# The last layer's weight split: high parts on ScalarE, low parts on GpSimd

## The chip, the cores and the metric

One core of one Trainium2 chip runs the whole program as one launch. The metric is the device time of the kernel in microseconds (us); shorter is better. Engines are called as in the profile: PE is TensorE, ACT is ScalarE, DVE is VectorE, POOL is GpSimd, and SPq is the queue from which SyncE issues transfers.

## The reference

Four layers run one after the other on x of 2 x 256 tokens by 512 columns. Each adds a cross attention and then a feed-forward block. The change touches only the last block, a feed-forward with 8-bit arithmetic and outlier columns:

```python
def _linear8bit(x, W, b):
    col_max = jnp.max(jnp.abs(x), axis=tuple(range(x.ndim - 1)))
    outlier = col_max > THRESHOLD
    x_in = jnp.where(outlier, 0.0, x)
    x_out = jnp.where(outlier, x, 0.0)
    y = _ste_quant_rows(x_in) @ _ste_quant_rows(W).T
    y = y + x_out @ W.T + b
    return y
h = _linear8bit(x, W1, b1)
return _linear8bit(h, W2, b2)
...
x = x + _L3_ffn_ref(_layernorm(x, axis=-1), L3_ffn_W1, L3_ffn_b1, L3_ffn_W2, L3_ffn_b2)
```

W1 is 2048 x 512 and W2 is 512 x 2048. The quantised product uses bf16 integers that were prepared earlier in the program. The outlier product `x_out @ W.T` is made in full precision.

## The kernel before

There is no scheduler: each engine runs a list of instructions that is written out by hand, and semaphores order the engines against each other. The last block is called f3 in the code.

A full-precision product is made of three passes. Each 512-wide operand is split into a high part (the value rounded to the matmul's format) and a low part (the value less its high part), and `passes` issues high x high, high x low and low x high; they are lines L326, L327 and L328. The activations' high parts come from ACT and their low parts from DVE. The weights of f3 come in eight chunks (cc = 0 to 7; 0 to 3 are W1, 4 to 7 are W2), each of 4 pieces of 128x512. Even chunks go to the buffers `wq_hi`/`wq_lo`, odd ones to `wo_hi`/`wo_lo`. Chunk 0 is split ahead of f3. Chunks 1 to 7 are split by POOL in `f3_pool`: `f3_split` makes the high part of a piece with a multiplication by one (L2065) and then its low part (L2067). POOL starts a chunk when the buffer of two chunks earlier is read for the last time: `out_full` counts the finished tiles of the first product, `used` those of the second.

PE's list (`f3_pe`) has the 16 tiles of the first outlier product, `out_first(j)`, each 12 matmuls into the banks ps_t; among them six of the 16 tiles of the integer product, `int_first(j)`, each 4 bf16 matmuls (L2145). Then 16 rounds follow, of which the first ten hold `int_first(6 + j)` and `out_second(j)`, and the last six only `out_second(j)`, 12 matmuls into ps_s. `int_first(j)` waits until DVE has read the integer tile of two before (`int_out`). `out_second(j)` waits for DVE's low part of activation tile j. Last come the 64 matmuls of the second integer product (L2192).

DVE's work on a tile is `tile(j)`, in this order: read the integer tile (L2299), keep the running maximum of two tiles before (`scale_kept`, L2296), add the two products (L2305), make the low part of the tile before (`outlier_lo(j - 1)`, L2270), and then the column maximum (L2309) and two masks (L2312, L2313).

ACT's list (`f3_act`) has `keep(j)`, which copies an outlier tile out of its bank (L2207), and `parts_of(j)`, which makes the high part `ho_hi` (L2213) and the magnitude `q_c` (L2216) of tile j and waits for the masks of tile j and, from tile 4 on, for `used` >= j - 3. `f3_norm_act` stands ahead of it and copies the turned, normalised x to `xF` (L2093).

Of the kernel before, what the change touches and what calls it, by code (L numbers as in the profile page):

```python
# [20 lines left out]
ALU = mybir.AluOpType  # L21
ACT = mybir.ActivationFunctionType
AX = mybir.AxisListType
F32 = mybir.dt.float32
# [43 lines left out]
def program(nc, A, out):  # L68
    ctx = ExitStack()
    with ctx:  # L70
# [4 lines left out]
        def at(name, shape, dt, kb):  # L75
            return nc.alloc_sbuf_tensor_at(name, shape, dt, offset=base + int(kb * KB))

        def sem(name):
            return ctx.enter_context(nc.semaphore(name))
# [6 lines left out]
        W = {"q": [at("wq_hi", [P, 4, 512], F32R, 64), at("wq_lo", [P, 4, 512], F32R, 72)],  # L86
             "o": [at("wo_hi", [P, 4, 512], F32R, 80), at("wo_lo", [P, 4, 512], F32R, 88)],
             "kv": [at("wkv_hi", [P, 4, 256], F32R, 96), at("wkv_lo", [P, 4, 256], F32R, 100)]}
# [159 lines left out]
        w_in = {r: sem(f"w_{r}_in") for r in ("q", "kv", "o", "f")}  # L248
        w_rdy = {r: sem(f"w_{r}_split") for r in ("q", "kv", "o", "f")}
# [123 lines left out]
        class Norm:  # L373
# [86 lines left out]
            def act(self, e):  # L460
                if self.i == 0:
                    for d in range(DK):
                        e.wait_ge(s_xfull, d + 1)
                        e.activation(xT[0][:, d, :], turn_banks[d][:, :], ACT.Copy).then_inc(s_xhi, 1)
                elif self.i == 7:
                    f3_norm_act(e)
                else:
                    turn_act(e, self.c.g, self.c.hi, xT, self.banks)
# [1121 lines left out]
        def f2_dve(e, link):  # L1590
# [30 lines left out]
            for half in range(2):  # L1621
# [9 lines left out]
        s3 = {n: sem(f"l3_{n}") for n in ("S", "max", "exp", "rec", "T", "thi", "tlo", "pv", "spread", "scaled", "ohi", "olo", "zero", "sel",  # L1631
                                         "job_full", "job_hi", "job_out")}
# [46 lines left out]
        L3_JOBS = len(jobs3)  # L1679
# [259 lines left out]
        def l3_dve(e, link):  # L1939
# [37 lines left out]
            for k in slots3:  # L1977
# [29 lines left out]
                for j in ended3.get(k - 1, ()):  # L2007
# [4 lines left out]
        cf = START["f3"]  # L2012
        s4 = {n: sem(f"f3_{n}") for n in ("x_mask", "x_kept",
                                         "out_full", "out_kept", "int_full", "int_out", "row_full", "row_out", "largest", "diag",
                                         "x_int", "summed", "masks", "h_scaled", "h_int", "h_int_dve", "kept_max", "magnitude", "x_magnitude", "hi", "lo", "used", "acc", "finished", "added", "dequantised", "outliers_added",
                                         "x_staged")}
        INT_BEHIND = {7: 0, 9: 1, 11: 2, 12: 3, 13: 4, 14: 5}
        EARLY = len(INT_BEHIND)
# [3 lines left out]
        def raw_of(cc):  # L2022

            return RAW["f"] if cc >= 2 and cc % 2 == 0 else RAW["o"]
# [33 lines left out]
        def f3_split(e, cc, piece):  # L2058
            role = "qo"[cc % 2]
            n = (cf.q, cf.o)[cc % 2] + cc // 2  # L2060
            if piece == 0:
                e.wait_ge(w_in[role], 16 * n + 16)
            w = raw_of(cc)[:, piece, :]
            hi, lo = W[role][0][:, piece, :], W[role][1][:, piece, :]
            e.tensor_tensor(hi, w, one[:, 0:1].to_broadcast([P, 512]), ALU.mult).then_inc(w_rdy[role], 1)  # L2065
            e.wait_ge(w_rdy[role], 8 * n + 2 * piece + 1)
            e.tensor_tensor(lo, w, hi.bitcast(F32), ALU.subtract).then_inc(w_rdy[role], 1)  # L2067

        def f3_pool(e):
            for cc in range(1, 8):  # L2070
                if cc == 1:
                    e.wait_ge(s3["job_full"], L3_JOBS)
                elif cc < 6:
                    e.wait_ge(s4["out_full"], 4 * (cc - 1))
                else:
                    e.wait_ge(s4["used"], 4 * (cc - 5))
                for piece in range(4):
                    f3_split(e, cc, piece)
            for i, t in enumerate(POOL_OUT):
                e.wait_ge(s4["dequantised"], i + 1)  # L2080
                e.tensor_tensor(x[:, t, :], x[:, t, :], q_c[:, t, :], ALU.add).then_inc(s4["added"], 1)
# [3 lines left out]
        acc_i = [ps_t[0][:, :], ps_t[1][:, :], ps_t[2][:, :], ps_o[:, :]]  # L2085

        def f3_norm_act(e):
            def hi(d):
                e.wait_ge(s4["x_mask"], 2 * d + 2)
                e.activation(xT[0][:, d, :], xF[:, d, :], ACT.Copy, scale=q_mo[:, d:d + 1]).then_inc(g_hi, 1)  # L2090
            for d in range(DK):
                e.wait_ge(g_full, cf.g - 4 + d + 1)
                e.activation(xF[:, d, :], turn_banks[d][:, :], ACT.Copy).then_inc(s4["x_kept"], 1)  # L2093
                if d:
                    hi(d - 1)
            hi(DK - 1)
# [99 lines left out]
        def f3_act(e):  # L2196
            for d in range(DK):
                e.activation(q_xm[:, d, :], xF[:, d, :], ACT.Abs, scale=q_mi[:, d:d + 1]).then_inc(s4["x_magnitude"], 1)
            e.wait_ge(s_lay, LAY["f3"])

            def row_copy(full, dst, bank):
                e.wait_ge(s4["row_full"], full)
                e.activation(dst[:, :], bank, ACT.Copy).then_inc(s4["row_out"], 1)

            def keep(j):
                e.wait_ge(s4["out_full"], j + 1)
                e.activation(h[:, j, :], out_bank[j % 2], ACT.Identity, bias=q_b1[:, j:j + 1]).then_inc(s4["out_kept"], 1)  # L2207

            def parts_of(j):
                e.wait_ge(s4["masks"], 2 * j + 2)  # L2210
                if j >= 4:
                    e.wait_ge(s4["used"], j - 3)
                e.activation(ho[0][:, j % 4, :], h[:, j, :], ACT.Copy, scale=q_mo[:, j:j + 1]).then_inc(s4["hi"], 1)  # L2213
                if j >= 4:
                    e.wait_ge(s4["kept_max"], j - 2)
                e.activation(q_c[:, j % 4, :], h[:, j, :], ACT.Abs, scale=q_mi[:, j:j + 1]).then_inc(s4["magnitude"], 1)  # L2216
            for j in range(4):
                keep(j)
            row_copy(3, q_srow, ring[3])
            row_copy(3, q_rrow, int_bank[0])  # L2220
            for j in range(4, 11):
                keep(j)
            parts_of(0)
            keep(11)
            keep(12)
            parts_of(1)
            keep(13)
            row_copy(4, q_s2row, ring[3])
            keep(14)
            parts_of(2)  # L2230
            keep(15)
            for j in range(3, HT):
                parts_of(j)
            row_copy(6, q_rrow, out_bank[1])
            n = 0
            for hb in range(HT):
                if hb in DVE_TILES:
                    continue
                n += 1
                e.wait_ge(s4["h_scaled"], n)  # L2240
                t = q_c[:, (n - 1) % 4, :]
                e.activation(t, t, ACT.Copy, bias=MAGIC).then_inc(s4["x_staged"], 1)
                e.wait_ge(s4["x_staged"], n)
                e.activation(hq[:, hb, :], t, ACT.Copy, bias=-MAGIC).then_inc(s4["h_int"], 1)
# [137 lines left out]
        def _(e):  # L2382
# [30 lines left out]
            l3_pool(e)  # L2413
            norms[7].pool(e)
            f3_pool(e)

        @block.tensor
# [25 lines left out]
        @block.scalar  # L2443
        def _(e):
            for b in range(B):
                e.wait_ge(s_ctx[b], 16)
                for d in range(DK):
                    c = slice(b * SK, (b + 1) * SK)
                    e.activation(cT[0][:, d, c], craw[:, d, c], ACT.Copy).then_inc(s_chi, 1)
                if b == 0:  # L2450
                    norms[0].act(e)
            a0.act(e)
            norms[1].act(e)
            f0_act(e)
# [134 lines left out]
```

## Time and profile before

| | |
|---|---|
| median of 3 runs | 2056.43 us (2055.41 to 2062.31) |
| profiled execution: its time | 2061.42 us |
| its span in the trace | 2059.6 us |
| last block, from the first outlier matmul to the end | 1914 to 2059.6 us |
| share of the span that PE is busy | 95% |

The profiled execution is one run of its own, so its time isn't one of the three. Times of single instructions below come from it, in us from the start of the span.

### The profile page before, as it was taken

How to read it: one execution, taken by the hardware profiler on the slowest of the kernel's cores; microseconds unless marked ns; L12 is line 12 of the kernel's file. 1: busy time of each engine (PE TensorE's matmuls, PEld its weight loads, DVE VectorE, ACT ScalarE, POOL GpSimd, SP SyncE). 2: the span in 40 equal slices, each digit the busy share in tenths (PEclk: the TensorE clock that was granted, in tenths of full speed). 3: DMA queues.
4: the chain of work that ended last, by engine and by line, in shares of the span. 5: the costliest groups of instructions: out<-in, count | busy, mean ns of one | idle time of the engine just before them, and what ended most of it. 6: DMA issues, size and time to landing. Idle time of an engine off the chain costs nothing.

```text
span 2059.6 us, 32190 instructions
## 1 busy us (share of the span) xinstructions
PE 1959.6 (95%) x11708; PEld 1662.0 (81%) x11716; DVE 1480.3 (72%) x2999; ACT 1112.6 (54%) x2315; POOL 843.1 (41%) x822
## 2 busy tenths in 40 slices
PE   6999999999899999988999999999998999998887
PEld 4888888888778888877888889889887877876665
DVE  6777777777676777666667767667676477777798
ACT  4756666566325555641556556555554167776333
POOL 6554654542633122043443253343215733151762
PEclk9999999999999999999999999999999999999899
DMA  4101111010213232012111121111111200120210
GB/s 154 52 22 52 52 41 43 21 52 21 90 29 81 74 91 56 23 39 72 42 44 55 42 67 55 41 67 60 43 47 41 99 23 22 42 83 1 71 57 21
DMA packets 49053, 107.56 MB, mean 52 GB/s; under 512 B 18560, under 2 KB 28032, under 8 KB 41600
## 3 DMA queue, kind: packets, MB, share of 16 engines
q1 hardware_dynamic: 35072, 84.51, 12.1%
q10 hardware_dynamic: 13824, 20.98, 3.3%
q8 instruction: 96, 1.57, 0.3%
q14 instruction: 61, 0.50, 0.1%
HBM read 97.08 MB, written 5.24 MB: 50 GB/s over the span
## 4 chain that ended last, share of the span: by engine, by line
PE 85%; DVE 8%; issue 2%; ACT 2%; POOL 2%; DMA 1%; SPq 0%; ACTq 0%; DVEq 0%; POOLq 0%
PE ps_s L326 11%; PE ps_s L328 11%; PE ps_s L327 11%; PE ps_t L1112 8%; PE ps_t L326 7%; PE ps_t L328 6%; PE ps_t L327 6%; PE ps_o L326 5%; PE ps_o L328 4%; PE ps_o L327 4%; PE ps_o L1854 3%; PE ps_t L1885 2%; PE ps_s L1840 2%; PE ps_t L1119 1%; DVE l_pt_lo L1240 1%
## 5 line engine op out<-in xcount | busy, mean ns | idle before, releaser
L1167 ACT ACTIVATE l_pt_hi<-ps_t 128x512 fp32r<-128x512 f32 (+1 forms) x512 | 244.7, 515 | 319.3 <-PE ps_t L1112 294.5
L1232 DVE TENSOR_REDUCE nmax<-ps_s 128x1 f32<-128x768 f32 x192 | 183.7, 957 | 232.3 <-PE ps_s L328 230.4
L1240 DVE TENSOR_TENSOR l_pt_lo<-ps_t,l_pt_hi 128x512 fp32r<-128x512 f32 (+1 forms) x512 | 281.6, 581 | 5.3 <-ACT l_pt_hi L1167 5.3
L1198 ACT ACTIVATE l_p<-ps_s,nmax 128x768 f32<-128x768 f32 x192 | 173.6, 904 | 150.3 <-DVE nmax L1232 149.6
L1112 PE MATMUL ps_t<-ident,l_p 128*128 128x128 f32 x1664 | 237.9, 274 | 10.6 <-DVE l_pt_lo L1240 5.2
L326 PE MATMUL ps_o<-l_pt_hi,l_v_hi 128*128 128x256 f32 (+1 forms) x832 | 236.8, 285 | 5.8 <-DVE l_pt_lo L1240 5.8
L1112 PEld LDWEIGHTS ps_t<-ident,l_p 128*128 128x128 f32 x1664 | 197.9, 141 | 53.3 <-issue 11.5
L328 PE MATMUL ps_o<-l_pt_hi,l_v_lo 128*128 128x256 f32 (+1 forms) x832 | 235.0, 282 | 0.0
L327 PE MATMUL ps_o<-l_pt_lo,l_v_hi 128*128 128x256 f32 (+1 forms) x832 | 234.6, 282 | 0.0
L326 PE MATMUL ps_s<-l_k_hi,l_q_hi 128*128 128x512 f32 (+3 forms) x512 | 206.7, 404 | 1.3 <-ACT l_p L1198 1.2
L364 POOL TENSOR_TENSOR wo_hi<-raw_big,one 128x512 fp32r<-128x512 f32 (+2 forms) x100 | 103.5, 1035 | 193.5 <-PE ps_t L328 181.7
L328 PE MATMUL ps_s<-l_k_hi,l_q_lo 128*128 128x512 f32 (+3 forms) x512 | 180.7, 353 | 0.0
L327 PE MATMUL ps_s<-l_k_lo,l_q_hi 128*128 128x512 f32 (+3 forms) x512 | 180.2, 352 | 0.0
L326 PEld LDWEIGHTS ps_o<-l_pt_hi,l_v_hi 128*128 128x128 f32 (+1 forms) x832 | 152.7, 184 | 13.4 <-DVE l_pt_lo L1240 11.1
L327 PEld LDWEIGHTS ps_o<-l_pt_lo,l_v_hi 128*128 128x128 f32 (+1 forms) x832 | 152.7, 184 | 2.3
L328 PEld LDWEIGHTS ps_o<-l_pt_hi,l_v_lo 128*128 128x128 f32 (+1 forms) x832 | 152.8, 184 | 0.0
L364 POOL TENSOR_TENSOR wq_hi<-raw_big,one 128x512 fp32r<-128x512 f32 (+1 forms) x104 | 114.8, 1104 | 90.1 <-PE ps_t L328 55.2
L652 POOL TENSOR_TENSOR w_raw<-w_raw,w_row 128x512 f32<-128x512 f32 x32 | 41.5, 1296 | 259.9 <-DMA w_raw<-in_f_w 215.4
L1228 DVE CUSTOM_DVE_ANT_0 l_p<-ps_s,l_mask 128x512 f32<-128x512 f32 x128 | 87.8, 686 | 81.9 <-PE ps_s L328 81.2
L1189 ACT ACTIVATE l_p<-l_p,rinv 128x768 f32<-128x768 f32 (+1 forms) x160 | 136.2, 852 | 1.2 <-DVE rinv L1293 0.5
L366 POOL TENSOR_TENSOR wq_lo<-raw_big,wq_hi 128x512 fp32r<-128x512 f32 (+1 forms) x104 | 132.6, 1275 | 8.2
L1297 DVE TENSOR_SCALAR l_p<-l_p,rinv 128x768 f32<-128x768 f32 (+1 forms) x160 | 130.8, 818 | 5.7
(397 smaller groups left out, 5375.1 us busy)
## 6 DMA issues: line engine op xcount, KB each, us to landing
raw_big<-in_l_wq SPq DMA_DIRECT2D x18, 1024.0 KB, 4.8
raw_big<-in_l_wo SPq DMA_DIRECT2D x18, 1024.0 KB, 4.8
w_raw<-in_f_w ACTq DMA_DIRECT2D x32, 256.0 KB, 3.1
raw_big<-in_f_w SPq DMA_DIRECT2D x7, 1024.0 KB, 4.9
raw_kv<-in_l_wkv SPq DMA_DIRECT2D x12, 512.0 KB, 5.7
raw_f<-in_f_w SPq DMA_DIRECT2D x4, 1024.0 KB, 4.8
w_nat<-in_f_w1n ACTq DMA_DIRECT2D x16, 256.0 KB, 3.0
w_nat<-in_f_w2n ACTq DMA_DIRECT2D x16, 256.0 KB, 3.0
```

Source lines behind the costliest of these rows:

```text
L326: pe.matmul(o, a[0], b[0], start=start, stop=False)
L327: pe.matmul(o, a[0], b[1], start=False, stop=False)
L328: return pe.matmul(o, a[1], b[0], start=False, stop=stop)
L364: pool.tensor_tensor(hi, w, one[0:parts, 0:1].to_broadcast([parts, cols]), ALU.mult).then_inc(w_rdy[role], 1)
L366: pool.tensor_tensor(lo, w, hi.bitcast(F32), ALU.subtract).then_inc(w_rdy[role], 1)
L1112: mm = e.transpose(o[:, kk * P:(kk + 1) * P], sp.p[:, k % 3, at:at + P], ident[:, :])
L1167: e.activation(sp.pt[u % 2][0][:, k0:k0 + nk, qt * P:(qt + 1) * P], ps_t[p % 2][:, 0:nk * P].rearrange("p (k q) -> p k q", q=P), ACT.Copy) ...
L1189: e.activation(pr, pr, ACT.Copy, scale=rinv[:, (k - 1) % TILES:(k - 1) % TILES + 1]).then_inc(s_scl[0], 1)
L1198: e.activation(sp.p[:, k % 3, :], sp.p[:, k % 3, :] if l.rope else self.scores_out(k), ACT.Exp, bias=nmax[:, i:i + 1], scale=-1.0 if l.rop ...
L1232: e.tensor_reduce(nmax[:, i:i + 1], self.scores_out(k), AX.X, ALU.max, negate=True).then_inc(s_max, 1)
L1240: e.tensor_tensor(pt[1], ps_t[p % 2][:, 0:nk * P].rearrange("p (k q) -> p k q", q=P), pt[0].bitcast(F32), ALU.subtract).then_inc(s_tlo, 1)
L1297: e.tensor_scalar(pr, pr, rinv[:, i:i + 1], None, ALU.mult).then_inc(s_scl[1], 1)
```

## The change

ACT gets a new function, `f3_weight_hi(e, cc)`, which makes the four high parts of chunk cc as copies and waits for what POOL used to wait for. It is called at seven places in ACT's list. POOL keeps the low parts, waits for each high part (`weight_hi`), and signals twice as much, so that every reader's count stays the same.

```diff
--- before.py
+++ after.py
...
@@ -2066,16 +2066,25 @@
             e.wait_ge(w_rdy[role], 8 * n + 2 * piece + 1)
             e.tensor_tensor(lo, w, hi.bitcast(F32), ALU.subtract).then_inc(w_rdy[role], 1)
 
+        def f3_weight_hi(e, cc):
+            role = "qo"[cc % 2]
+            if cc == 1:
+                e.wait_ge(s3["job_full"], L3_JOBS)
+            elif cc < 6:
+                e.wait_ge(s4["out_full"], 4 * (cc - 1))
+            else:
+                e.wait_ge(s4["used"], 4 * (cc - 5))
+            e.wait_ge(w_in[role], 16 * ((cf.q, cf.o)[cc % 2] + cc // 2) + 16)
+            for piece in range(4):
+                e.activation(W[role][0][:, piece, :], raw_of(cc)[:, piece, :], ACT.Copy).then_inc(s4["weight_hi"], 1)
+
         def f3_pool(e):
             for cc in range(1, 8):
-                if cc == 1:
-                    e.wait_ge(s3["job_full"], L3_JOBS)
-                elif cc < 6:
-                    e.wait_ge(s4["out_full"], 4 * (cc - 1))
-                else:
-                    e.wait_ge(s4["used"], 4 * (cc - 5))
+                role = "qo"[cc % 2]
                 for piece in range(4):
-                    f3_split(e, cc, piece)
+                    e.wait_ge(s4["weight_hi"], 4 * (cc - 1) + piece + 1)
+                    e.tensor_tensor(W[role][1][:, piece, :], raw_of(cc)[:, piece, :],
+                                    W[role][0][:, piece, :].bitcast(F32), ALU.subtract).then_inc(w_rdy[role], 2)
             for i, t in enumerate(POOL_OUT):
                 e.wait_ge(s4["dequantised"], i + 1)
                 e.tensor_tensor(x[:, t, :], x[:, t, :], q_c[:, t, :], ALU.add).then_inc(s4["added"], 1)
@@ -2085,6 +2094,8 @@
         acc_i = [ps_t[0][:, :], ps_t[1][:, :], ps_t[2][:, :], ps_o[:, :]]
 
         def f3_norm_act(e):
+            f3_weight_hi(e, 1)
+
             def hi(d):
                 e.wait_ge(s4["x_mask"], 2 * d + 2)
                 e.activation(xT[0][:, d, :], xF[:, d, :], ACT.Copy, scale=q_mo[:, d:d + 1]).then_inc(g_hi, 1)
@@ -2218,10 +2229,15 @@
                 keep(j)
             row_copy(3, q_srow, ring[3])
             row_copy(3, q_rrow, int_bank[0])
-            for j in range(4, 11):
+            f3_weight_hi(e, 2)
+            for j in range(4, 8):
+                keep(j)
+            f3_weight_hi(e, 3)
+            for j in range(8, 11):
                 keep(j)
             parts_of(0)
             keep(11)
+            f3_weight_hi(e, 4)
             keep(12)
             parts_of(1)
             keep(13)
@@ -2229,8 +2245,11 @@
             keep(14)
             parts_of(2)
             keep(15)
+            f3_weight_hi(e, 5)
             for j in range(3, HT):
                 parts_of(j)
+                if j in (7, 11):
+                    f3_weight_hi(e, 6 + j // 8)
             row_copy(6, q_rrow, out_bank[1])
             n = 0
             for hb in range(HT):
```

ACT's list around tiles 14, 15 and 3 is one of the two places that matter below. `h` is what `keep` writes, `ho_hi` and `q_c` are what `parts_of` writes. Before:

```order
L2207 ACTIVATE h<-ps_t,q_b_183 128x512 [waits f3_out_full]
L2213 ACTIVATE ho_hi<-h,q_mo 128x512 [waits f3_masks]
L2216 ACTIVATE q_c<-h,q_mi 128x512
L2207 ACTIVATE h<-ps_t,q_b_183 128x512 [waits f3_out_full]
L2213 ACTIVATE ho_hi<-h,q_mo 128x512 [waits f3_masks]
L2216 ACTIVATE q_c<-h,q_mi 128x512
L2213 ACTIVATE ho_hi<-h,q_mo 128x512 [waits f3_used,f3_masks]
```

The same place in ACT's list of the changed kernel, where L2218 is `keep` and L2224 and L2227 are `parts_of`:

```order
L2218 ACTIVATE h<-ps_t,q_b_183 128x512 [waits f3_out_full]
L2224 ACTIVATE ho_hi<-h,q_mo 128x512 [waits f3_masks]
L2227 ACTIVATE q_c<-h,q_mi 128x512
L2218 ACTIVATE h<-ps_t,q_b_183 128x512 [waits f3_out_full]
L2079 ACTIVATE wo_hi<-raw_big 128x512 [waits w_o_in,f3_out_full]
L2079 ACTIVATE wo_hi<-raw_big 128x512 x3
L2224 ACTIVATE ho_hi<-h,q_mo 128x512 [waits f3_masks]
L2227 ACTIVATE q_c<-h,q_mi 128x512
L2224 ACTIVATE ho_hi<-h,q_mo 128x512 [waits f3_used,f3_masks]
```

The four copies of chunk 5 now stand between `keep(15)` and `parts_of(3)`.

POOL's list at chunk 5, before:

```order
L2065 TENSOR_TENSOR wo_hi<-raw_big,one 128x512 [waits w_o_in,f3_out_full]
L2067 TENSOR_TENSOR wo_lo<-raw_big,wo_hi 128x512 [waits w_o_split]
L2065 TENSOR_TENSOR wo_hi<-raw_big,one 128x512
L2067 TENSOR_TENSOR wo_lo<-raw_big,wo_hi 128x512 [waits w_o_split]
L2065 TENSOR_TENSOR wo_hi<-raw_big,one 128x512
L2067 TENSOR_TENSOR wo_lo<-raw_big,wo_hi 128x512 [waits w_o_split]
L2065 TENSOR_TENSOR wo_hi<-raw_big,one 128x512
L2067 TENSOR_TENSOR wo_lo<-raw_big,wo_hi 128x512 [waits w_o_split]
```

POOL's whole part of f3's weights in the changed kernel, chunks 1 to 7:

```order
L2086 TENSOR_TENSOR wo_lo<-raw_big,wo_hi 128x512 [waits f3_weight_hi,xn_ready]
L2086 TENSOR_TENSOR wo_lo<-raw_big,wo_hi 128x512 [waits f3_weight_hi] x3
L2086 TENSOR_TENSOR wq_lo<-raw_f,wq_hi 128x512 [waits f3_weight_hi] x4
L2086 TENSOR_TENSOR wo_lo<-raw_big,wo_hi 128x512 [waits f3_weight_hi] x4
L2086 TENSOR_TENSOR wq_lo<-raw_f,wq_hi 128x512 [waits f3_weight_hi] x4
L2086 TENSOR_TENSOR wo_lo<-raw_big,wo_hi 128x512 [waits f3_weight_hi] x4
L2086 TENSOR_TENSOR wq_lo<-raw_f,wq_hi 128x512 [waits f3_weight_hi] x4
L2086 TENSOR_TENSOR wo_lo<-raw_big,wo_hi 128x512 [waits f3_weight_hi] x4
```

Of POOL's 56 instructions on these weights 28 are left, one for each piece.

## Rows read from the trace of the kernel before

**Rows 1.** The page: engines' busy time, share of the span, instructions.
```profile
PE 1959.6 (95%) x11708; PEld 1662.0 (81%) x11716; DVE 1480.3 (72%) x2999; ACT 1112.6 (54%) x2315; POOL 843.1 (41%) x822
```

**Rows 2.** Busy time of each engine in three stretches of f3, granted clock.
```profile
core 0: us, PE busy (x) PEld busy (x) DVE busy (x) ACT busy (x) POOL busy (x), PEclk, DMA share, GB/s
1949.00:1967.00 18.00, 17.86 (x83) 13.23 (x84) 15.54 (x22) 6.31 (x11) 16.60 (x12) 1.00 0.18 59
1970.00:1982.20 12.20, 8.50 (x37) 5.62 (x37) 12.13 (x16) 4.58 (x7) 11.53 (x8) 1.00 0.04 18
1982.20:1989.20 7.00, 6.74 (x30) 4.76 (x30) 6.93 (x15) 1.34 (x2) 0.00 (x0) 1.00 0.47 153
```

**Rows 3.** Timeline of PE: start, duration; the integer tiles and the closing transposes.
```profile
1970.16 1.04 PE L2145 MATMUL ps_t<-xq,q_w 128*128 128x512 bf16 x4
...
1975.41 1.04 PE L2145 MATMUL ps_o<-xq,q_w 128*128 128x512 bf16 x4 [1.46 <-DVE q_t L2299]
...
1981.36 1.04 PE L2145 MATMUL ps_t<-xq,q_w 128*128 128x512 bf16 x3 [2.15 <-DVE q_t L2299]
...
1985.42 1.04 PE L2145 MATMUL ps_o<-xq,q_w 128*128 128x512 bf16 x4 [0.26 <-DVE q_t L2299]
...
1989.04 1.04 PE L2145 MATMUL ps_t<-xq,q_w 128*128 128x512 bf16 x4
...
1999.02 0.81 PE L2145 MATMUL ps_t<-xq,q_w 128*128 128x512 bf16 x3 [2.29 <-DVE q_t L2299]
...
2004.02 1.04 PE L2145 MATMUL ps_o<-xq,q_w 128*128 128x512 bf16 x4
...
2011.49 1.04 PE L2145 MATMUL ps_o<-xq,q_w 128*128 128x512 bf16 x3
...
2028.70 0.60 PE L2115 MATMUL ps_t<-ident,q_amx 128*128 128x128 f32 x4
```

**Rows 4.** Two DVE lines over f3: durations ns min/median/max.
```profile
L2296 DVE TENSOR_TENSOR q_amx<-q_c,q_amx x16: 679/968/1406, 1956.4 to 2026.5; 128x512 f32<-128x512 f32 x16
...
L2305 DVE TENSOR_TENSOR h<-q_t,h x16: 678/1280/1789, 1949.9 to 2022.9; 128x512 f32<-128x512 f32 x16
```

**Rows 5.** Timeline of DVE around tiles 5 to 8.
```profile
1974.62 0.74 DVE L2299 SCALAR_TENSOR_TENSOR q_t<-ps_o,q_sw,q_srow 128x512 f32<-128x512 f32 x1
...
1980.56 0.74 DVE L2299 SCALAR_TENSOR_TENSOR q_t<-ps_t,q_sw,q_srow 128x512 f32<-128x512 f32 x1
...
1984.63 0.74 DVE L2299 SCALAR_TENSOR_TENSOR q_t<-ps_o,q_sw,q_srow 128x512 f32<-128x512 f32 x1
...
1986.49 0.74 DVE L2270 SCALAR_TENSOR_TENSOR ho_lo<-h,q_mo,ho_hi 128x512 fp32r<-128x512 f32 x1
...
1987.99 0.74 DVE L2299 SCALAR_TENSOR_TENSOR q_t<-ps_t,q_sw,q_srow 128x512 f32<-128x512 f32 x1
```

**Rows 6.** Timeline of ACT and DVE at tile 3.
```profile
1970.75 0.71 ACT L2213 ACTIVATE ho_hi<-h,q_mo 128x512 fp32r<-128x512 f32 x1
...
1972.07 1.78 DVE L2270 SCALAR_TENSOR_TENSOR ho_lo<-h,q_mo,ho_hi 128x512 fp32r<-128x512 f32 x1
```

**Rows 7.** Timeline of ACT: four copies from SBUF; first instruction of f3.
```profile
9.66 2.19 ACT L2449 ACTIVATE cT_hi<-craw 128x512 fp32r<-128x512 f32 x4 [7.64 <-DMA craw<-in_ctxT]
...
1909.35 0.60 ACT L2093 ACTIVATE xF<-ps_t 128x512 f32<-128x512 f32 x1 [13.02 <-PE ps_t L487]
```

**Rows 8.** Timeline of POOL: one low part.
```profile
1930.46 1.28 POOL L2067 TENSOR_TENSOR wq_lo<-raw_f,wq_hi 128x512 fp32r<-128x512 f32 x1
```

**Rows 9.** ACT's waits in f3: total us, times, longest.
```profile
ACT h L2207 <- PE ps_t L328: 33.3, 16, 3.0
...
ACT ho_hi L2213 <- PE ps_s L328: 17.6, 6, 4.8
```

**Rows 10.** Timeline of DVE: first low part of x, at the start of f3.
```profile
1911.71 1.72 DVE L2101 SCALAR_TENSOR_TENSOR xT_lo<-xF,q_mo,xT_hi 128x512 fp32r<-128x512 f32 x1
```

**Rows 11.** Busy time and granted clock around integer tile 12.
```profile
2000.00:2003.40 3.40, 3.40 (x10) 2.68 (x9) 3.37 (x6) 0.00 (x0) 1.04 (x1) 0.52 0.00 0
```

More of the change, by code:

```diff
@@ L2014, in program @@
                                          "out_full", "out_kept", "int_full", "int_out", "row_full", "row_out", "largest", "diag",
-                                         "x_int", "summed", "masks", "h_scaled", "h_int", "h_int_dve", "kept_max", "magnitude", "x_magnitude", "hi", "lo", "used", "acc", "finished", "added", "dequantised", "outliers_added",
+                                         "x_int", "weight_hi", "summed", "masks", "h_scaled", "h_int", "h_int_dve", "kept_max", "magnitude", "x_magnitude", "hi", "lo", "used", "acc", "finished", "added", "dequantised", "outliers_added",
                                          "x_staged")}
```

## The prediction

> **What bounds the kernel now.** I read the page first: PE is busy for 95% of the span [rows 1], so only a place where PE waits can pay. Then the busy time by stretch, in f3 alone, since nothing else is touched. From 1949 to 1967 PE is busy 17.86 of 18 us, though POOL runs for 16.60 of them [rows 2]: there PE is the bound, and what POOL or DVE gain is worth nothing. From 1970.0 to 1982.2 PE is busy 8.50 of 12.2 us, and DVE 12.13, with POOL on for 11.53. From 1982.2 to 1989.2 POOL is silent, and PE is busy 6.74 of 7 us [rows 2]. So the rounds behind 1970 are bound by DVE while POOL works, and by PE while it rests.
>
> PE's timeline gives the size. A round with nothing to wait for takes 1989.04 - 1985.42 = 3.62 us [rows 3]. The ten integer tiles of the rounds start at 1970.16 to 2011.49, nine rounds apart, 41.33 us where 9 x 3.62 = 32.58 would do: PE loses 8.75 us. Three rows name DVE's read of an integer tile (L2299) as what ended the wait [rows 3]. The last six rounds have no integer tile and run on without a wait. 8.75 us is therefore the ceiling for this stage.
>
> Why DVE is slow there: its two adds take 0.68 us at best and 1.41 and 1.79 at worst [rows 4]. Tile 5 (1974.62 to 1980.56), with POOL on, takes 5.94 us; tile 7 (1984.63 to 1987.99), with POOL off, 3.36 [rows 5]. PE wants a tile every 3.62 us, so DVE is quick enough alone and too slow beside POOL. Under POOL it loses 2.58 of 5.94 us, 0.43 us for each us. The three chunks split in this stage (5, 6, 7) have POOL on for some 11.5 us each [rows 2], 34.5 us, so DVE loses about 15.
>
> **The change part by part.** Removed: 28 multiplications on POOL, 12 of them in the stage that counts. Left there are 12 lows, 1.28 us each undisturbed [rows 8]; beside a busy DVE I take 1.6, 6.4 us a chunk instead of 11.5. At the same 0.43 DVE loses 3 x 6.4 x 0.43 = 8.3 us instead of 15, so it gets about 6.7 back. PE gets only what of it lies where PE waits.
>
> That price is weighed against a rule. The Trainium skill (SBUF — State Buffer, "Who interferes with whom") says that a VectorE instruction with two SBUF inputs and a GpSimd instruction lock each other out for their whole length. By it a low can cost DVE its full duration; at 1.28 us that makes 12 x 1.28 = 15.4 us, and the relief would be nil. The rows lie between: of the 3.36 us of a tile some 1.9 (L2296, L2305 and L2270) go to instructions with two SBUF inputs, and lows that run beside the rest cost nothing.
>
> Added: 28 copies on ACT. Four copies of 128x512 out of SBUF took 2.19 us at the program's start [rows 7]; this price I use for each chunk. Six of the seven groups are covered. Chunk 1 stands where ACT sat idle for 13.02 us [rows 7]. Chunks 2, 3 and 4 stand in front of a `keep`, and ACT waited there for PE before all 16 of them, 33.3 us in total and up to 3.0 at once [rows 9]; an outlier tile is needed two tiles later, so even 1 us of delay would be hidden. Chunks 6 and 7 stand in front of a `parts_of` that waited for PE's `used`, 17.6 us in 6 waits [rows 9], 2.9 on average. Without that cover each would cost up to 2.2 us.
>
> Chunk 5 is not covered. It stands in front of `parts_of(3)`, which ran at 1970.75 without a wait, and DVE used its result at 1972.07 [rows 6]. Now `ho_hi` of tile 3 begins near 1970.75 + 2.19 = 1972.9 and ends 0.71 later, at 1973.65. DVE's low part of tile 3 moves from 1972.07 to 1973.65 or, if a POOL instruction is ahead of it, 1974.0. Queued behind it are the column maximum and masks of tile 4 and the read of integer tile 5: from the start of L2270 to the next L2299 it is 1987.99 - 1986.49 = 1.50 us undisturbed [rows 5], 1.9 with some of POOL. So that read starts at about 1975.9 instead of 1974.62, 1.3 us late, and PE's 1975.41 becomes 1976.7. Bounds: 0.4 (POOL out of the way at once) and 2.2 us (all four copies).
>
> Then the relief begins. POOL's four lows of chunk 5 end near 1977.4 instead of 1982.0. Tile 5 costs 3.36 + 1.5 x 0.43 = 4.0, so DVE reads tile 6 at 1979.9, and PE's round starts at 1980.7 instead of 1981.36: 0.6 ahead. The next is then bound by PE, 3.62 later at 1984.4 instead of 1985.42: 1.0 ahead. Rounds follow at 1988.0 and 1991.6. `used` for chunk 6 comes at 1988.0; `ho_hi` of tile 7 is done by 1989.0, and DVE reads tile 9 at 1989.0 + 1.50 = 1990.5. Chunk 6 lays 6.4 us of POOL on the next tile: 3.36 + 6.4 x 0.43 = 6.1, so tile 10 is read from 1996.6 and PE goes on at 1997.4 instead of 1999.02: 1.6 ahead.
>
> The next round cost 2004.02 - 1999.02 = 5.00 us [rows 3], 1.38 more than 3.62, because from 2000.0 to 2003.4 the granted clock was 0.52, TensorE's lower level of 1.2 GHz [rows 11]. PE had waited 2.29 us just before. Now it waits 1997.4 - (1991.6 + 3.62) = 2.2 us, against 1999.02 - 1992.66 - 3.62 = 2.7 worked out the same way before. Waits of 1.46 and 2.15 us [rows 3] had no such fall behind them. I take it that it doesn't come back, which adds 1.4: 3.0 ahead. Chunk 7 meets a DVE that is a tile ahead; 0.2 more. This stage gives 3.2 us.
>
> At the start of f3, x's first low part took 1.72 us beside POOL [rows 10], where the same kind of instruction takes 0.74 alone [rows 5]. POOL now has half the work there; of the 0.98 us I take 0.3, with 0 and 0.98 as bounds. Weight loads are issued earlier, since a chunk's split ends earlier; nothing waited for one.
>
> Sum: -3.2 - 0.3 = -3.5 us on a profiled execution of 2061.42 us, or 0.17%. That execution lies 5.0 above the median 2056.43, nearly all of it outside this question, so I apply the difference to the median: 2052.9 us. A measurement of this kernel can tell about 0.3%, 6.2 us, from no change.
>
> **The rivals.** (1) PE's waits all go: DVE gets more than 6.7 back, the delay at chunk 5 costs nothing, and the start gives all it can. -8.75 - 0.98 = -9.7, 2046.7 us. For it speaks that DVE alone needs 3.36 for PE's 3.62; against it that the lows still come in one burst a chunk. Half of this way (6.2 or more) would be measurable: 0.16.
>
> (2) The clock falls again behind the wait near 1996: 1.6 + 0.2 + 0.3 = 2.1 ahead, 2054.3 us; a chance of 0.3, beside 0.38 for the forecast itself. Both lie in the same class. The Trainium skill (TensorE: Matmul & The Clock Gate, "HAM oscillation — how this bites in real kernels") has waits of PE throw it back to the slow clock, which agrees with the trace as far as that fall after a wait goes.
>
> (3) Slower: ACT's queue. The copies of chunk 5 cost their full 2.2 us in front of tile 3, and the lows block DVE as much as highs and lows did, so that the relief of the rounds is nil. Then the end moves by +2.2 less 0.3, 2058.3 us. It decides where the relief up to the next PE-bound round is under the delay: I have 1.9 (from 1.3 behind to 0.6 ahead) against 1.3. Against it speaks that tile 7 was quick as soon as POOL stopped [rows 5], and POOL now stops earlier. The lock of the Trainium skill's SBUF — State Buffer page, above, would lead here. 0.12, and of this 0.05 beyond the measurable, if chunks 6 and 7 lose their cover too (up to 2.2 each, +6.3 in all).
>
> (4) The change does nothing, because the lows are as long as POOL's presence was: 2056.4, a chance of 0.04.
>
> **How the numbers follow.** The forecast, (2), (4) and the nearer part of (3) are within 0.3%: 0.38 + 0.3 + 0.04 + 0.07 = 0.79. Faster by over 0.3%: 0.16. Slower: 0.05. The range reaches from near rival (1) to near rival (3): 2047.5 to 2058.5.
>
> **What would show it.** Right: lows of 1.28 to 1.6 us on POOL, four a chunk, no highs; ACT's four copies in about 2.2 us; `ho_hi` of tile 3 some 2 us after `keep(15)`, with DVE idle for 1 to 2 us in front of its low part; DVE's adds at 0.68 us in more of the tiles; PE's waits in the rounds 5 to 6 us in total instead of 8.75. Wrong: DVE's tile beside lows still near 5.9 us, ACT waiting for a weight load, copies over 0.65 us apart, or a stretch at 0.5 of the clock in another place of f3, which costs or gives back 1.4 to 3 us.

## The result and the profile after

The changed kernel takes 2053.28 us (median of 20 runs, 2048.43 to 2057.46), the kernel before 2058.43 us in the runs beside it (20 runs, 2053.48 to 2062.31). The ratio is 0.9977 with a 95% interval of 0.9969 to 0.9984: 4.7 us or 0.23% faster (3.3 to 6.4 us). The forecast was 3.5 us, 0.17%. That the time itself was forecast at 2052.9 us, 0.4 from the measured one, is luck: it was worked out from 2056.43 us for the kernel before, which the 20 runs put at 2058.43. A second series of 10 runs gave 0.9982 (0.9973 to 0.9991).

The profiled execution after has a span of 2055.2 us and a time of 2057.14 us. Its page shows POOL's busy time down from 843.1 us [rows 1] to 805.5, and DVE's from 1480.3 to 1465.1, though DVE has the same instructions. This is the page's part 1, busy time, share of the span and instructions:

```profile
PE 1960.3 (95%) x11708; PEld 1662.8 (81%) x11716; DVE 1465.1 (71%) x2999; ACT 1126.2 (55%) x2343; POOL 805.5 (39%) x794
```

PE's timeline answers to [rows 3]; L487 is the first transpose of x, L326 the first outlier matmul, L2156 an integer tile, L2126 the closing transposes. Start, duration, and in brackets the idle time ahead with what ended it:

```profile
1909.24 2.82 PE L487 MATMUL ps_t<-ident,xn 128*128 128x128 f32 x12 [5.92 <-DVE xn L416]
...
1913.74 0.76 PE L326 MATMUL ps_t<-xT_hi,wq_hi 128*128 128x512 f32 x1 [0.82 <-DVE xT_lo L2112]
...
1940.21 0.81 PE L2156 MATMUL ps_t<-xq,q_w 128*128 128x512 bf16 x3
...
1968.37 1.04 PE L2156 MATMUL ps_t<-xq,q_w 128*128 128x512 bf16 x4
...
1974.38 1.11 PE L2156 MATMUL ps_o<-xq,q_w 128*128 128x512 bf16 x4 [2.22 <-DVE q_t L2318]
...
1979.60 1.04 PE L2156 MATMUL ps_t<-xq,q_w 128*128 128x512 bf16 x3
1983.21 1.04 PE L2156 MATMUL ps_o<-xq,q_w 128*128 128x512 bf16 x4
...
1996.14 0.81 PE L2156 MATMUL ps_t<-xq,q_w 128*128 128x512 bf16 x3 [1.84 <-DVE q_t L2318]
1999.56 1.04 PE L2156 MATMUL ps_o<-xq,q_w 128*128 128x512 bf16 x4
...
2006.85 1.04 PE L2156 MATMUL ps_o<-xq,q_w 128*128 128x512 bf16 x3
...
2024.10 0.60 PE L2126 MATMUL ps_t<-ident,q_amx 128*128 128x128 f32 x4
```

From integer tile 6 to the closing transposes it is 2024.10 - 1968.37 = 55.73 us, against 2028.70 - 1970.16 = 58.54 before [rows 3]: 2.8 us less. The nine rounds take 38.48 us, so the loss against 9 x 3.62 us is down from 8.75 to 5.9. The first two rounds are the odd ones: the first takes 6.01 us (5.25 before), the second 5.22 (5.95 before).

The timelines of ACT, POOL and DVE show why; L2079 is a group of ACT's copies of a chunk, L2224 `ho_hi`, L2086 POOL's lows, L2289 DVE's low part of a tile, L2318 its read of an integer tile, L2324 the add. They answer to [rows 5, 6]. ACT first:

```profile
1968.96 2.18 ACT L2079 ACTIVATE wo_hi<-raw_big 128x512 fp32r<-128x512 f32 x4
...
1971.04 0.71 ACT L2224 ACTIVATE ho_hi<-h,q_mo 128x512 fp32r<-128x512 f32 x1
```

POOL's lows in the same view:

```profile
1969.72 5.45 POOL L2086 TENSOR_TENSOR wo_lo<-raw_big,wo_hi 128x512 fp32r<-128x512 f32 x4 [9.07 <-ACT wo_hi L2079]
1989.11 6.36 POOL L2086 TENSOR_TENSOR wq_lo<-raw_f,wq_hi 128x512 fp32r<-128x512 f32 x4 [13.95 <-ACT wq_hi L2079]
```

And DVE's timeline at tile 3 and at the tile beside chunk 6:

```profile
1971.79 1.03 DVE L2289 SCALAR_TENSOR_TENSOR ho_lo<-h,q_mo,ho_hi 128x512 fp32r<-128x512 f32 x1 [2.27 <-ACT ho_hi L2224]
...
1989.38 0.74 DVE L2318 SCALAR_TENSOR_TENSOR q_t<-ps_o,q_sw,q_srow 128x512 f32<-128x512 f32 x1
...
1990.88 1.77 DVE L2324 TENSOR_TENSOR h<-q_t,h 128x512 f32<-128x512 f32 x1
...
1995.12 0.74 DVE L2318 SCALAR_TENSOR_TENSOR q_t<-ps_t,q_sw,q_srow 128x512 f32<-128x512 f32 x1
```

The four copies take 2.18 us and `ho_hi` of tile 3 stands right behind them; DVE idles 2.27 us for it. POOL is on for 5.45 and 6.36 us a chunk instead of 11.5 [rows 2]. Beside the lows of chunk 6 DVE's tile still takes 1995.12 - 1989.38 = 5.74 us: a tile full of lows is as slow as one beside highs and lows (5.94, [rows 5]), but it is one tile and not two.

The stage that surprised is the start of f3. From the first transpose to integer tile 0 it is 1940.21 - 1909.24 = 30.97 us, against 33.88 in the profile before; I had forecast a gain of 0.3.

**Two profiles of one kernel differ.** In every one of the 14 profiles the clock of PE falls to half (1.2 GHz) for stretches of a few us, and not at the same place. In this profile one stretch lies over the second round (the view of stretches: busy us of PE, PEld, DVE, ACT and POOL, the count of instructions behind each, then the granted clock, the DMA share and GB/s):

```profile
1976.00:1977.00 1.00, 1.00 (x4) 0.71 (x4) 1.00 (x3) 0.00 (x0) 0.00 (x0) 0.50 0.79 131
```

So I read every experiment by its stages, and by the clock in them.

| profile | A: transposes to integer tile 0 | B: rounds | C: from B's end to the end |
|---|---|---|---|
| before | 33.88 | 58.54 | 30.9 |
| before_again | 32.90 | 59.55 | 30.0 |
| after | 30.97 | 55.73 | 31.1 |
| after_again | 30.73 | 55.79 | 31.0 |
| chunk1_only | 30.95 | 58.43 | 29.9 |
| chunks567_only | 32.76 | 54.69 | 32.4 |
| parts3_first | 30.98 | 55.46 | 31.5 |
| lows_8_columns | 30.96 | 53.72 | 30.4 |
| pool_keeps_highs_too | 30.74 | 58.52 | 31.1 |
| pool_after_x_lows | 33.60 | 58.55 | 31.0 |
| piecewise | 30.75 | 53.75 | 30.4 |
| piecewise_again | 31.08 | 53.73 | 30.8 |
| piecewise_late_chunk1 | 35.40 | 53.72 | 29.9 |
| chunk5_in_halves | 30.73 | 53.72 | 32.3 |

Each is the difference of two starts in PE's timeline, as worked out above, in us; C is the span less the start of the closing transposes. The first transpose of x starts anywhere from 1901.0 to 1911.0 us in these profiles, after code that is the same in all of them. That spread, and the 2.5 us in C, are in every time; A and B are not touched by it. Where the row of a tile's integer matmuls reads x3 and 0.81 us instead of x4 and 1.04, the trace lacks its first matmul and the start reads 0.23 us late. This makes A 0.23 us too long in before, after, chunk1_only, chunks567_only, parts3_first and lows_8_columns: for the changed kernel 30.74 and 30.73 us are left in its two profiles.

### The profile page after: what moved, and what is told of

The parts are those of the page before. It is cut to its first block and busy times, and to the rows that moved or that the text cites. A ratio compares the mean times of both kernels' runs of the same rounds, so it can differ in the third digit from the quotient of the medians.

```text
span 2055.2 us, 32218 instructions
## 1 busy us (share of the span) xinstructions
PE 1960.3 (95%) x11708; PEld 1662.8 (81%) x11716; DVE 1465.1 (71%) x2999; ACT 1126.2 (55%) x2343; POOL 805.5 (39%) x794
## 5 line engine op out<-in xcount | busy, mean ns | idle before, releaser
L326 PE MATMUL ps_o<-l_pt_hi,l_v_hi 128*128 128x256 f32 (+1 forms) x832 | 236.3, 284 | 6.0 <-DVE l_pt_lo L1240 6.0
L326 PE MATMUL ps_s<-l_k_hi,l_q_hi 128*128 128x512 f32 (+3 forms) x512 | 206.5, 403 | 1.3 <-ACT l_p L1198 1.2
L326 PEld LDWEIGHTS ps_o<-l_pt_hi,l_v_hi 128*128 128x128 f32 (+1 forms) x832 | 152.3, 183 | 13.6 <-DVE l_pt_lo L1240 11.3
```

Of the source, the lines that this page charges most:

```text
L326: pe.matmul(o, a[0], b[0], start=start, stop=False)
```

## The experiments

**chunk1_only** and **chunks567_only** each keep part of the change. The edit (the second has `(5, 6, 7)`); other chunks are split by POOL as before:

```diff
+        ON_ACT = (1,)
+
         def f3_weight_hi(e, cc):
+            if cc not in ON_ACT:
+                return
...
+                if cc not in ON_ACT:
...
+                    for piece in range(4):
+                        f3_split(e, cc, piece)
+                    continue
```

> Only chunk 1's four highs are on ACT; chunks 2 to 7 are split by POOL as before. The profiled pair shows the first outlier stage (from the transposes of x to integer tile 0) 2.9 us shorter after the change. Theory A (POOL's highs at the start delayed x's low parts on DVE, worth about 0.3 us, and the rest of the 2.9 is where TensorE's slow stretch happened to lie): from the first transpose of x to integer tile 0 this kernel takes 0.3 to 1 us less than before at the same clock, and the time is 0 to 1.5 us under before. Theory B (chunk 1 alone brings the whole 2.9 us, by the clock or by DVE): the time is about 3 us under before, ratio 0.9985. The rounds keep all of their 8.75 us of waits in both.

> Only the highs of chunks 5, 6 and 7 are on ACT; chunks 1 to 4 are split by POOL as before. Theory A (the gain of the rounds comes from less POOL beside DVE): from integer tile 6 to the closing transposes 55.7 us as in the changed kernel, against 58.5 before, so 2.8 us less, ratio about 0.9986. Rival (the earlier chunks matter for the rounds too, since they let DVE run ahead): more than 57 us in the rounds.

Measured: 2056.89 us, ratio 0.9992 (0.9983 to 1.0001), and 2055.85 us, ratio 0.9991 (0.9982 to 1.0). By the clocks both are near the edge of what can be told; the stages are clear. Chunk 1 alone gives A = 30.95, the whole gain of the start, and leaves B at 58.43. Chunks 5 to 7 alone give B = 54.69, and leave A at 32.76. So the change has two parts that add up, and chunks 2 to 4 give nothing to B. For chunk 1 the truth lies between the theories: 1.8 us of A (32.76 - 30.95) are POOL's doing, more than the 0.3 to 1 of theory A and less than the whole 2.9 of theory B.

The gain of A can be followed step by step. In chunks567_only PE waits for each of x's low parts, with a full clock from the first outlier matmul on. PE's timeline at the start of f3:

```profile
1909.44 0.47 PE L326 MATMUL ps_t<-xT_hi,wq_hi 128*128 128x512 f32 x1 [1.77 <-DVE xT_lo L2126]
...
1910.85 0.50 PE L326 MATMUL ps_t<-xT_hi,wq_hi 128*128 128x512 f32 x1 [0.48 <-DVE xT_lo L2126]
...
1912.54 0.50 PE L326 MATMUL ps_t<-xT_hi,wq_hi 128*128 128x512 f32 x1 [0.72 <-DVE xT_lo L2126]
...
1913.99 0.50 PE L326 MATMUL ps_t<-xT_hi,wq_hi 128*128 128x512 f32 x1 [0.49 <-DVE xT_lo L2126]
```

The first matmul comes 1909.44 - 1904.00 = 5.44 us behind the first transpose; in the changed kernel it is 1913.74 - 1909.24 = 4.50. That is 0.94 us, nearly the whole of the upper bound of 0.98 that I had. The rest comes behind it. DVE's timeline of chunks567_only has x's four low parts, the last two in one row:

```profile
1907.59 1.71 DVE L2126 SCALAR_TENSOR_TENSOR xT_lo<-xF,q_mo,xT_hi 128x512 fp32r<-128x512 f32 x1
...
1910.06 0.74 DVE L2126 SCALAR_TENSOR_TENSOR xT_lo<-xF,q_mo,xT_hi 128x512 fp32r<-128x512 f32 x1
...
1911.56 2.38 DVE L2126 SCALAR_TENSOR_TENSOR xT_lo<-xF,q_mo,xT_hi 128x512 fp32r<-128x512 f32 x2
```

In the changed kernel they take 0.84, 0.93 and 1.62 us. So the second low part was not slow with all of POOL's work there, but the first, the third and the fourth were. The four maxima of x, which DVE makes next, take 3.17 us against 2.87. When PE transposes the maxima, the whole difference is there. The rows are from PE's timelines of chunks567_only and of chunk1_only:

```profile
1917.87 0.66 PE L2140 MATMUL ps_s<-ident,q_amx 128*128 128x128 f32 x4 [0.18 <-DVE q_amx L2311]
```

```profile
1923.02 0.66 PE L2140 MATMUL ps_s<-ident,q_amx 128*128 128x128 f32 x4
```

They stand 1917.87 - 1904.00 = 13.87 and 1923.02 - 1910.95 = 12.07 us behind the first transpose, 1.80 apart. In both profiles of the changed kernel it is 12.07 us too, wherever the slow stretch lies. And 1.1 us more of the first pair's 2.9 (33.88 - 32.76) is only where the slow stretch lay: the kernel before has been profiled twice, with 33.88 and 32.90.

This pair also mends a reading of mine. I had put the long round at integer tile 12 (5.00 us, [rows 3]) down to the slow clock there [rows 11]. In chunk1_only the same round has a full clock and takes 2003.73 - 1998.91 = 4.82 us, with a wait for DVE. This is the stretch of that round in chunk1_only, with the columns as above:

```profile
1998.90:2003.70 4.80, 3.57 (x15) 2.45 (x14) 4.77 (x8) 1.10 (x3) 1.98 (x2) 1.00 0.00 0
```

PE's timeline of the same profile, at the end of the round:

```profile
2003.73 1.04 PE L2170 MATMUL ps_o<-xq,q_w 128*128 128x512 bf16 x4 [1.24 <-DVE q_t L2332]
```

DVE bound that round too. The tiles' rows at 1999.02 [rows 3] and 1998.91 both lack their first matmul, so that the rounds are really 5.23 and 5.05 us: a slow stretch that fell where PE would wait anyway cost 0.2 us.

**lows_8_columns** takes the lows away as well, all but 8 columns of each in chunks 5 to 7:

```diff
-                    e.tensor_tensor(W[role][1][:, piece, :], raw_of(cc)[:, piece, :],
-                                    W[role][0][:, piece, :].bitcast(F32), ALU.subtract).then_inc(w_rdy[role], 2)
+                    n = 512 if cc < 5 else 8
+                    e.tensor_tensor(W[role][1][:, piece, 0:n], raw_of(cc)[:, piece, 0:n],
+                                    W[role][0][:, piece, 0:n].bitcast(F32), ALU.subtract).then_inc(w_rdy[role], 2)
```

> The changed kernel, but POOL makes only 8 of the 512 columns of each low part of chunks 5, 6 and 7, so that part of the low products is left out and POOL is all but gone from the rounds; ACT's copies stay. Theory A (POOL's presence is what slows DVE's tile): DVE's adds take 0.68 us in every tile, a tile 3.36 us, and of PE's waits only the one behind chunk 5's copies is left, about 1.5 us: 51.5 to 52.5 us from integer tile 6 to the closing transposes, against 55.7. Rival (ACT's copies hold up the tiles too, at chunks 6 and 7): over 53 us, with PE waits near integer tiles 11 to 13.

Measured: 2049.87 us, ratio 0.9959 (0.9946 to 0.9971), B = 53.72. One slow stretch lies in the second round, which takes 5.22 us for 3.62; without it B would be 52.1 by estimate, in the expected range. The view of the add's line (durations in ns, min/median/max):

```profile
L2325 DVE TENSOR_TENSOR h<-q_t,h x16: 682/684/1762, 1940.6 to 2008.3; 128x512 f32<-128x512 f32 x16
```

And the one wait of PE over 1 us in the rounds, in PE's timeline:

```profile
1970.10 1.04 PE L2157 MATMUL ps_o<-xq,q_w 128*128 128x512 bf16 x4 [1.94 <-DVE q_t L2319]
```

The median add is 684 ns, against 1280 before [rows 4]. What is left is the wait behind chunk 5's copies. ACT's copies of chunks 6 and 7 cost nothing, as forecast.

**pool_keeps_highs_too** gives POOL the highs back as doubles, with ACT's copies in place:

```diff
+                    if cc >= 5:
+                        e.tensor_tensor(W[role][1][:, piece, :], raw_of(cc)[:, piece, :],
+                                        one[:, 0:1].to_broadcast([P, 512]), ALU.mult).then_inc(s4["again"], 1)
+                        e.wait_ge(s4["again"], 4 * (cc - 5) + piece + 1)
```

> The changed kernel, in which POOL also repeats the high part of each piece of chunks 5, 6 and 7 (a multiplication by one of the same size, written where the low part goes a moment later). ACT's copies stay where they are. Theory A (what the rounds gain is POOL's missing half beside DVE): the relief goes, PE waits in rounds 2 and 3 and near integer tiles 12 and 13 as before, and with the delay of tile 3 by ACT's copies the rounds take 59 to 60.5 us at full clock, more than the 58.5 of before. Rival (the gain came from ACT making the highs sooner, not from POOL's absence): 54.7 to 56 us. The start keeps its gain in both.

Measured: 2058.1 us, ratio 0.9996 (0.9985 to 1.0008). B is 58.52, the value of before: with the highs on POOL again the whole gain of the rounds is gone, though ACT makes them as early as in the changed kernel. The rival falls. I had expected 59 to 60.5, the delay at tile 3 on top; it wasn't there in the sum: the second integer tile comes 5.87 us behind the first (5.25 in the kernel before), and the later rounds make up for it.

**parts3_first** asks for the price of the copies' place:

```diff
-            f3_weight_hi(e, 5)
-            for j in range(3, HT):
+            parts_of(3)
+            f3_weight_hi(e, 5)
+            for j in range(4, HT):
```

> The changed kernel with parts_of(3) ahead of chunk 5's copies. Theory A (the copies delayed DVE's low part of tile 3 and with it integer tile 7): DVE no longer idles 2.3 us there, the second round starts 1.5 to 2.2 us earlier relative to the first than 6.0 us, and the stage to the closing transposes is 1 to 2 us shorter than 55.7 us. Rival (POOL's lows would then stand beside DVE's low part and take it back): the stage stays within 0.4 us of 55.7.

Measured: 2053.11 us, ratio 0.9971 (0.9957 to 0.9984), B = 55.46. Theory A was half right. The second round now starts 3.65 us behind the first instead of 6.01, 2.4 earlier, but the wait stands one round later:

```profile
1973.87 1.04 PE L2156 MATMUL ps_t<-xq,q_w 128*128 128x512 bf16 x3 [1.96 <-DVE q_t L2319]
```

That is the burst of four lows, which now all stand beside DVE's tile. The stage gains 0.27 us, inside the rival's 0.4; a slow stretch lies in the third round here and in the second round of the changed kernel, so this is not a clean comparison. Without the stretches B would be some 53.9 us here (a round of 3.62 for 5.21) against the 54.69 of chunks567_only. By this estimate the order of `parts_of(3)` and the copies is worth 0.8 us: less than theory A, but more than the rival's 0.4.

**piecewise** (and **piecewise_again**, the same kernel) also spreads chunks 6 and 7:

```diff
+        def weight_hi_piece(e, cc, piece):
+            role = "qo"[cc % 2]
+            e.wait_ge(s4["used"], 4 * (cc - 6) + piece + 1)
...
-                if j in (7, 11):
-                    f3_weight_hi(e, 6 + j // 8)
+                if 4 <= j < 12:
+                    weight_hi_piece(e, 6 + (j - 4) // 4, j % 4)
```

> The changed kernel with parts_of(3) ahead of chunk 5's copies, and the copies of chunks 6 and 7 spread: one piece behind each of parts_of(4) to parts_of(11), as soon as its buffer is read out, so that POOL's lows come one per round. Theory A (a burst of four lows makes one DVE tile take 5.7 us, which PE must wait for; one low a tile costs DVE 0.4 to 1.1 us of the 3.64 that a round has, 3.36 are needed): the wait of 1.84 us at integer tile 12 goes, no round over 4.1 us but the third, 52 to 53.5 us for the rounds at full clock. Rival (one low a tile blocks DVE by up to a whole low, 1.28 us, so that every round is DVE-bound): 8 rounds of 4.2 to 4.6 us, 56 us or more.

> The kernel that spreads the copies, once more, beside the changed kernel in the same call. By the profiles its rounds are 2 to 2.6 us shorter than those of the changed kernel at equal clock, so its ratio should be some 0.001 under that one's: about 0.9965, and its first time of 0.9958 partly luck.

Measured: 2049.93 us, ratio 0.9958 (0.9943 to 0.9974), and 2053.47 us, ratio 0.9973 (0.9962 to 0.9983), beside after_again at 0.9982 in the runs next to it. B is 53.75 and 53.73: the wait at integer tile 12 is gone, the last six rounds take 3.64 or 3.65 us each, 2 us less than the changed kernel in both profiles. By the times alone the two kernels' intervals overlap, so that it beats the changed kernel is shown by the stage and only likely by the clock. I had expected 52 to 53.5 at full clock. What I missed stands in the second profile, where no slow stretch lies in the rounds:

```profile
1974.02 1.04 PE L2162 MATMUL ps_t<-xq,q_w 128*128 128x512 bf16 x4 [1.93 <-DVE q_t L2325]
...
1979.23 1.04 PE L2162 MATMUL ps_o<-xq,q_w 128*128 128x512 bf16 x4 [1.41 <-DVE q_t L2325]
```

The first pieces of chunk 6 follow right on chunk 5's burst, and DVE is bound for a second round.

**chunk5_in_halves** moves the pieces of chunks 6 and 7 one tile later and cuts that burst in two:

```diff
-            f3_weight_hi(e, 5)
+            weight_hi_piece(e, 5, 0)
+            weight_hi_piece(e, 5, 1)
...
+                if j == 4:
+                    weight_hi_piece(e, 5, 2)
+                    weight_hi_piece(e, 5, 3)
```

> As the kernel that spreads the copies of chunks 6 and 7, which come one tile later, and chunk 5's copies in two pairs, behind parts_of(3) and parts_of(4). Theory A (the wait of 2 us at integer tile 8 comes from four lows of chunk 5 in one burst): it falls to under 1 us, and the rounds take 51.5 to 52.5 us at full clock, up to 1.6 more where a slow stretch of the clock falls in them. Rival (the lows only move, and DVE has no slack left in rounds 2 to 6): the same loss appears as small waits over several rounds, and the stage is not shorter than 53.7 us less the slow stretch, 52.1.

Measured: 2053.62 us, ratio 0.9972 (0.9962 to 0.9982), B = 53.72. The wait did not shrink: POOL's two pairs of lows came 0.32 us apart and filled the same tile.

```profile
1968.01 3.00 POOL L2092 TENSOR_TENSOR wo_lo<-raw_big,wo_hi 128x512 fp32r<-128x512 f32 x2 [10.30 <-ACT wo_hi L2085]
1971.33 3.05 POOL L2092 TENSOR_TENSOR wo_lo<-raw_big,wo_hi 128x512 fp32r<-128x512 f32 x2 [0.32 <-ACT wo_hi L2085]
```

The next round, 5.21 us, has a slow stretch in this profile. DVE is busy for 4.48 us of it, against 5.17 of 5.21 in piecewise_again, so by estimate it would be 0.7 us shorter or more at full clock; no profile shows it, and it stays open.

**pool_after_x_lows** tries the start without ACT, from the kernel before:

```diff
                     e.wait_ge(s3["job_full"], L3_JOBS)
+                    e.wait_ge(g_free, cf.g)
```

> The kernel before, with one wait more: POOL begins chunk 1 only when DVE has made the four low parts of x. All highs stay on POOL, nothing is added to ACT. Theory A (the start was slow because POOL's instructions stood beside x's low parts): from the first transpose to the first outlier matmul 4.4 to 4.5 us instead of 5.45, and 30.9 us to integer tile 0 at full clock against 32.8, as with the highs on ACT; chunk 1 is still done in time. Rival (POOL now collides with the later maxima and DVE's rounding of x): less than 1 us of it remains. The rounds stay at 58.4 to 58.5 us.

Measured: 2062.64 us, ratio 1.0017 (1.0008 to 1.0026), which is 3.5 us slower. The first outlier matmul does come 4.49 us behind the first transpose, as theory A had it, but A is 33.60: the rival was right. POOL's chunk 1 now stands beside the four running maxima of x, which DVE makes next, and PE waits for them. DVE's timeline of pool_after_x_lows, and then PE's:

```profile
1913.38 5.92 DVE L2279 TENSOR_TENSOR q_amx<-q_xm,q_amx 128x512 f32<-128x512 f32 x4
```

```profile
1919.35 0.66 PE L2116 MATMUL ps_s<-ident,q_amx 128*128 128x128 f32 x4 [2.94 <-DVE q_amx L2279]
```

In the changed kernel the same four take 2.87 us, in DVE's timeline:

```profile
1918.38 2.87 DVE L2297 TENSOR_TENSOR q_amx<-q_xm,q_amx 128x512 f32<-128x512 f32 x4
```

The stages don't account for the 3.5 us: A is only 0.7 us longer than the 32.90 of before_again, and B is the same. The profiled execution is the fastest of the 11 of this kernel (2057.89 us); what the others lost besides is not shown.

**piecewise_late_chunk1** has the same wait on top of piecewise.

> As the kernel that spreads the copies, and POOL also waits for the four low parts of x before it begins chunk 1. Expected beside it: the first transpose to the first outlier matmul 0.1 us less (DVE's low part 0.74 instead of 0.84 us), to integer tile 0 0.1 to 0.3 us less, the rounds the same. By the rival (a later start of POOL pushes chunk 1's lows into other DVE work that counts) the stage to integer tile 0 is longer than 30.97.

Measured: 2054.1 us, ratio 0.998 (0.9969 to 0.9991), with A = 35.40 and B = 53.72: the rival again, PE waits 3.24 us for the maxima. Here a slow stretch lies right behind that wait (granted clock 0.50 from 1922 to 1924 us), which makes A longer than in pool_after_x_lows, where the clock was full. Where the lows stand matters as much as how many they are.

**before_again** and **after_again** are the two kernels unchanged.

> The kernel before, unchanged, for a second profile. Theory A (where TensorE's slow stretches lie differs from one execution to the next; the rest doesn't): 58.4 to 58.6 us for the rounds without a slow stretch, up to 1.6 more with one; 32.7 to 34 us from the first transpose to integer tile 0, by where the slow stretch lies.

> The changed kernel, unchanged, for a second profile and more times. Theory A: 54.7 us for the rounds without a slow stretch, 55.7 with one as in the first profile; 30.7 to 31 us from the first transpose to integer tile 0 wherever the slow stretch lies; ratio 0.9970 to 0.9985.

Measured: 2061.72 us in one run, and 2056.92 us, ratio 0.9982 (0.9973 to 0.9991). In before_again a slow stretch lies in the third round, so B is 59.55 and not 58.5, while the round at integer tile 12 takes 2005.16 - 2000.12 = 5.04 us at full clock. In after_again B is 55.79, with a slow stretch in the second round as in the first profile, and A is 30.73, as expected. The two stretches, with the columns as above:

```profile
1981.50:1986.80 5.30, 5.24 (x16) 3.70 (x16) 5.23 (x10) 0.72 (x2) 0.75 (x1) 0.68 0.56 202
2000.10:2005.20 5.10, 3.82 (x17) 2.61 (x18) 5.07 (x8) 1.40 (x4) 2.21 (x2) 1.00 0.00 0
```

## Why the prediction was right, point by point

**What bounds the stage** held. B's gain comes and goes with POOL's highs alone (54.69 without them, 58.52 with doubles of them), and PE's long waits ended with DVE's read in all of these profiles.

**The rounds**: forecast -3.2 us; -2.8 in the profile, and -3.7 where no slow stretch mixes in (54.69 against 58.43). That the profile's value came so near is luck in part, as the clock below shows. The loss of DVE beside a low was near the 0.43 taken: 5.74 - 3.36 = 2.4 us for 6.36 us of lows, 0.37. My sum had 6.1 us for that tile. So the first sign that I had named for being wrong, a tile beside lows near 5.9 us, was no sign: the sum itself asked for it. The signs for being right came: copies of 2.18 us, adds with a median of 0.69 us instead of 1.28, 5.9 us lost in the rounds where 5 to 6 was said. DVE idled for 2.27 us, a little over the 1 to 2.

**Chunk 5's copies in front of tile 3** did what was said: DVE's low part began 1971.79 - 1968.37 = 3.4 us behind integer tile 6 instead of 1.9, 1.5 later (1.6 to 1.9 forecast). At PE it cost 0.8 us (6.01 against 5.25), where 1.3 was said, inside the bounds of 0.4 and 2.2. The cover of the six other groups held: four copies took 2.18 us against 2.19, and in lows_8_columns no PE wait over 0.15 us stands near chunks 6 and 7.

**The clock** was the step that failed. I booked 1.4 us as the cost of a slow stretch at integer tile 12 that would not come back. The stretch had cost some 0.2 us, since the round takes 4.82 and 5.04 us at full clock: DVE bound it. The 1.4 us were gained all the same, from DVE, and a slow stretch in the second round of the changed kernel took 1.05 back (5.22 us against 4.17 in chunks567_only). Two errors of about the same size, with opposite signs, and that they cancel is luck. Rival (2) had the right event in the wrong place: the clock fell behind a wait of 2.2 us in the second round, in both profiles of the changed kernel, and not near 1996.

**The start** was mis-sized: 0.3 us taken, 1.8 measured. I priced the first of x's four low parts only, and took a third of its bound. The third and fourth were slow beside POOL as well, and so were the maxima a little, and PE waited for them. The bound of 0.98 was therefore no bound of the term.

The sum from these: 3.7 + 1.8 = 5.5 us, or 4.5 with the slow stretch of the second round, against 4.7 in the times (3.3 to 6.4). The forecast of 3.5 fell short by the start.

## What to carry to other kernels

Work on GpSimd that nobody waited for was paid for by VectorE where the two met, so price a helper by where it stands beside the bound engine, not by its own wait. When it is moved, ask which instruction of VectorE it will meet next: a later start of the same work made this kernel slower (ratio 1.0017). And before a long round is put down to TensorE's slow clock, look whether another engine bound it; a second profile of the same kernel answers that cheaply.

## What the runs showed of the hardware

The same four maxima of 128x512 on DVE, with both inputs in SBUF, took 2.87 us without POOL and 5.92 us beside it, a factor of 2.1. DVE's reads of the integer tiles, whose first input is in PSUM, stayed at 0.74 us in either case. But the rounding of x, with one input in SBUF, was slow too: 1.40 us beside POOL and 0.43 without. The view of what writes and reads `q_t` in the kernel before (ns, min/median/max):

```profile
L2299 DVE SCALAR_TENSOR_TENSOR q_t<-ps_t,q_sw,q_srow x8: 740/742/751, 1949.1 to 2016.6; 128x512 f32<-128x512 f32 x8
...
L2266 DVE TENSOR_SCALAR xq<-q_t x4: 428/1398/1400, 1933.3 to 1941.2; 128x512 bf16<-128x512 f32 x4
```

The Trainium skill (SBUF — State Buffer, "Who interferes with whom") says that a VectorE instruction meets GpSimd if it has two SBUF inputs, against a GpSimd instruction that reads SBUF, or if it runs in a mode that uses two ports. The trace agrees with the first; the slow rounding fits the second, but no run here shows its mode. By the same page of the Trainium skill the instruction that starts first has the lock, so it can delay either engine. My reading in the prediction, that each low costs DVE its full length, took one side of it only, and the relief would have been nil; the rounds gained 3.7 us. Beside chunk 6 both lost: the tile took 5.74 us for 3.36, and four lows took 6.36 us, 1.59 each, for 1.28 undisturbed.

Slow stretches of PE's clock began at different places in profiles of one kernel. In the rounds each of them began behind a wait of PE of 1.9 to 2.3 us, in 10 of the 14 profiles; waits of the same length had none behind them in the other four (2.13 and 2.30 us in chunk1_only, 2.22 in chunks567_only, 1.93 in piecewise_again, 1.94 in piecewise_late_chunk1). A stretch cost 1.1 us in a round where PE was the bound but for a short wait (59.55 against 58.43 for B), by estimate 1.6 us where PE did not wait at all (5.22 for 3.62 in lows_8_columns), and 0.2 us in the round at integer tile 12, which DVE bound (5.23 against 5.05).
